# One more chunk of a weight product on ScalarE and two small copies on GpSimd in a graph network kernel

## What is computed

```python
def hyp_agg(x, src, dst, w, c, n_nodes):
    xt = logmap0(x, c)
    msg = xt[src] * w[:, None]
    agg = jax.ops.segment_sum(msg, dst, num_segments=n_nodes)
    return proj(expmap0(agg, c), c)
```

## Time and profile before

| | |
|---|---|
| Median of 3 runs | 1208.23 us (1206.75 to 1208.87) |
| The profiled execution, its own time | 1208.75 us |
| Its span, first to last instruction | 1206.9 us |
| TensorE busy | 1038.3 us (86%) |
| VectorE busy | 998.4 us (83%) |
| ScalarE busy | 668.8 us (55%) |
| GpSimd busy | 27.6 us (2%) |

### The profile page before, as it was taken

The page is one execution under the profiler, slowest core; times in us unless marked ns, Lnnn a source line. Parts: engine busy times, 40 slices in busy tenths (PEclk is TensorE's granted clock), DMA queues, the critical chain, the costliest instruction groups (busy, mean ns, idle before and its releaser), DMA issues.

```text
span 1206.9 us, 53493 instructions
## 1 busy us (share of the span) xinstructions
PE 1038.3 (86%) x22006; PEld 960.3 (80%) x22006; DVE 998.4 (83%) x1478; ACT 668.8 (55%) x1837; POOL 27.6 (2%) x28
## 2 busy tenths in 40 slices
PE   2079888898989898638996679999999999999997
PEld 2058778787777777437996569999999999999997
DVE  8889999999999999275665868888888888888884
ACT  5348888888888888310001565555555555555552
POOL 7000000000000000100000000000000000000000
PEclk9579999999999999859997779999999999999999
DMA  2002232323232322759940345444444444444440
GB/s 80 0 33 117 101 124 93 124 93 124 93 124 93 124 101 116 317 204 335 422 166 30 104 139 172 149 155 160 157 158 158 158 157 158 157 152 159 151 147 28
DMA packets 44875, 169.96 MB, mean 141 GB/s; under 512 B 19440, under 2 KB 19766, under 8 KB 44827
## 3 DMA queue, kind: packets, MB, share of 16 engines
q1 hardware_dynamic: 44827, 169.28, 38.7%
HBM read 121.11 MB, written 48.14 MB: 140 GB/s over the span
## 4 chain that ended last, share of the span: by engine, by line
PE 52%; DVE 33%; issue 8%; DVEq 4%; ACT 2%; DMA 0%; POOL 0%; POOLq 0%; ACTq 0%
PE PS L1507 17%; PE PS L1509 11%; PE PS L1382 8%; DVE arena L1008 7%; PE PS L1527 7%; DVE arena L985 5%; PE PS L1522 5%; DVE arena L993 4%; DVE arena L971 3%; DVE arena L980 2%; DVEq L354 2%; PE PS L1461 1%; PE PS L1413 1%; DVE Cw L799 1%; DVE rows L799 1%
## 5 line engine op out<-in xcount | busy, mean ns | idle before, releaser
L1507 PE MATMUL PS<-arena 125*128 125x128 bf16 x3600 | 343.8, 219 | 6.3 <-ACT RT L736 6.2
L1507 PEld LDWEIGHTS PS<-arena 125*128 125x128 bf16 x3600 | 249.9, 97 | 11.2 <-issue 6.9
L1382 PE MATMUL PS<-arena,A 125*64 125x72 f32 x4800 | 180.4, 231 | 72.3 <-DVE aggTw L1019 40.8
L1382 PEld LDWEIGHTS PS<-arena,A 125*64 125x64 f32 x4800 | 166.5, 139 | 81.7 <-issue 29.1
L631 ACT ACTIVATE arena<-arena 128x72 bf16<-128x72 bf16 x864 | 216.9, 343 | 2.1 <-DVE arena L993 2.1
L750 ACT ACTIVATE arena<-PS 128x512 bf16<-128x512 f32 (+2 forms) x336 | 171.9, 543 | 82.8 <-PE PS L1509 82.8
L743 ACT ACTIVATE arena<-arena 128x512 bf16<-128x512 f32 x144 | 90.8, 631 | 152.8 <-DVE arena L1226 152.7
L1509 PE MATMUL PS<-arena 108*128 108x128 bf16 x1200 | 166.9, 220 | 0.0
L1509 PE MATMUL PS<-arena,HTw 108*128 108x128 bf16 x1200 | 165.8, 219 | 0.0
L1367 PE MATMUL PS<-arena 128*128 128x72 bf16 x3600 | 126.7, 199 | 0.0
L1367 PEld LDWEIGHTS PS<-arena 128*128 128x128 bf16 x3600 | 120.7, 100 | 4.9
(11 more groups left out here) (189 smaller groups left out, 1340.0 us busy)
## 6 DMA issues: line engine op xcount, KB each, us to landing
adjacency<-arena SPq DMA_DIRECT2D x48, 900.0 KB, 3.6
arena<-adjacency SPq DMA_DIRECT2D x46, 900.0 KB, 7.6
Bw<-slot_rows SPq DMA_DIRECT2D x48, 800.0 KB, 4.1
Cw<-slot_rows SPq DMA_DIRECT2D x48, 700.0 KB, 4.3
arena<-q_table SPq DMA_DIRECT2D x144, 18.0 KB
q_table<-arena SPq DMA_DIRECT2D x6, 336.0 KB
slot_rows<-slot_row SPq DMA_DIRECT2D x49, 13.0 KB
x_sb<-in_x SPq DMA_DIRECT2D x1, 700.0 KB
```

The lines of the kernel that those rows point to most:

```text
L1382: last = mm(sums[half, :], A[:, b, :], adjacency[0:PN, b, :], start=(b < 2), stop=(b >= NB - 2))
L1507: mm(ps, OTs[k][:, b, :], P3[:, b, part, :], start=(part == 0), stop=False)
```

## The change

ScalarE multiplies the third weight part of all 25 buckets (25 instructions a group, before 18), and VectorE's product of 128x504 elements goes away. ScalarE no longer makes the two small copies out of PSUM; GpSimd makes them from `slots`, once `slots_set` is counted, and counts `copied`. `third_weights(g)` waits for `copied` of group g in place of `slots_set`. `third_set` counts four chunks a group where it counted three, and TensorE waits for it before each chunk.

```diff
+            def copy_slots(g, k):
+
+                pool.wait_ge(slots_set, nth(g))
+                if from_third(g):
+                    pool.wait_ge(third_set, nth(len(CHUNKS) * (g - 2) + len(CHUNKS) - 1))
+                nc.gpsimd.tensor_copy(slot_dst[:, bass.ds(g, 1), :, :].rearrange("p g b d -> p (g b) d"),
+                                      slots[k][:, 1, 0:NB, :])
+                nc.gpsimd.tensor_copy(third[k], slots[k][:, 4, 0:NB, 0]).then_inc(copied, 1)
+
+            fast = in_order(pool, 0)
+            with pool.If(fast == 1):
+                copy_slots(0, 0)
+                copy_slots(1, 1)
+                with pool.Fori(1, NG // 2) as j:
+                    copy_slots(2 * j, 0)
+                    copy_slots(2 * j + 1, 1)
@@ take_slots
                 sc.wait_ge(onehots_set, nth(g - 2))
-                nc.scalar.activation(slot_dst[:, bass.ds(g, 1), :, :].rearrange("p g b d -> p (g b) d"),
-                                     slots_ps[:, 1, 0:NB].unsqueeze(2).broadcast_to([128, NB, 2]), ACT.Copy)
-                nc.scalar.activation(third[k], slots_ps[:, 4, 0:NB], ACT.Copy)
+                sc.wait_ge(copied, nth(g - 2))
@@ third_weights
-                sc.wait_ge(slots_set, nth(g))
+                sc.wait_ge(copied, nth(g))
                 sc.wait_ge(dst1_set, nth(g))
                 sc.wait_ge(blocks_done[-1], nth(g - 2))
-                for bs in CHUNKS[1:]:
+                for bs in CHUNKS:
@@ slot_destinations
-                ve.wait_ge(third_set, nth(3 * g - 1))
+                ve.wait_ge(third_set, nth(len(CHUNKS) * g - 1))
@@ slot_weights
-                for c, n in ((2, CB), (0, NB), (1, NB)):
+                for c, n in ((0, NB), (1, NB)):
@@ blocks
-                    if c:
-                        pe.wait_ge(third_set, nth(3 * g + c - 1))
+                    pe.wait_ge(third_set, nth(len(CHUNKS) * g + c))
```

More of the change, by code:

```diff
@@ L274, in gnn_kernel @@
         dst1_set, onehots_set, third_set = counts("dst1_set"), counts("onehots_set"), counts("third_set")
+        copied = counts("copied")
         blocks_done, blocks_set = (counts(n, len(CHUNKS)) for n in ("blocks_done", "blocks_set"))
```

## The result

The change makes the kernel **slower**: 1292.31 us in the median of 4 runs (1285.94 to 1295.92) against 1208.55 for the kernel before in the same comparison (4 runs), a ratio of 1.068 with a 95% interval of 1.063 to 1.0736. The forecast was 1269, with a range of 1258 to 1300: right in direction and inside the range, 23 us too low at its middle. The profiled execution took 1295.92 us, its span is 1294.2, 87.3 more than before.

A forecast was written before the change was run, and what follows sets the result against it. VectorE (8.523 us a group) bounds the loop now; ScalarE would at 8.23 + 1.73 - 0.16 = 9.80. 46 groups add 58.7 us, the first interval 1.6: +60.3, about 1269 us, range 1258 to 1300.

The forecast's parts named there:

- forecast's own range: Range of the main case, ScalarE bounding the loop with hidden GpSimd copies: 1260 to 1278 us, chance 65%.
- GpSimd held twice: Rival, 15%: both GpSimd copies wait behind VectorE instructions, 3.5 us in all, 14 us more, about 1283 us.
- the clock: Rival, 5%: TensorE's clock falls through longer idleness, slowing blocks; 65 us more if each time, about 1334 us.
- ScalarE's circle: ScalarE's work and waits between runs of products in the loop: from 8.23 to 9.80 us a group, above VectorE's 8.19.
- Seven more products at 0.247 each: Added products on ScalarE in each loop group, between two engine answers: 1.73 us more a group.
- TensorE's new wait for the first chunk's products: TensorE's wait for third_set ahead of the first chunk of blocks: hidden, costs nothing.
- the sum: 58.7 us for 46 groups plus 1.6 for the first interval: +60.3 us on 1208.75, giving 1269.0 us.
- The copies on GpSimd: The two small copies in each group, ending about 1.7 us after the slots if held once: hidden, 0 us.
- cover: Time from the slots' copy to ScalarE's next products, in which GpSimd's copies can hide: 3.26 us.
- GpSimd gets in nowhere: Rival, 10%: GpSimd's copies get no turn until VectorE's add_sums; 101 us more, about 1370 us.
- The first copy: GpSimd's first copy, in the first group: 0.96 us extra once, covered by ScalarE's 2.06 us wait for VectorE.
- Not slower (3%): Rival, 3%: added ScalarE products overlap more deeply and cost little; 15.5 us less, about 1193 us.

The follow-up runs named there:

- kernel with the filled idle time: The changed kernel plus 24 unread 128x128 matrix products on TensorE between first_apply and slot_rows in each group; 1273.65 us (ratio 1.054).
- kernel with the copies alone: The kernel before with only the two small copies moved to GpSimd, ScalarE still multiplying 18 buckets and VectorE the first chunk; 1250.52 us (ratio 1.0331).
- kernel with the pause for GpSimd: The kernel with the copies alone, but VectorE's slot_destinations waits for GpSimd's copied of its own group instead of slots_set; 1228.20 us (ratio 1.0136).

## Why the prediction was right, and where it was short

- **Inside the range, in part by luck.** 1292.31 us lies outside the forecast's own range of 1260 to 1278. It lies inside 1258 to 1300 because that range had been widened for GpSimd held twice, a case whose 14 us did not come; the clock, whose case the range left out for the most part, took the room.
- **ScalarE's circle as the new bound: right, and exact.** Forecast 9.80 us, measured 9.82. *Seven more products at 0.247 each*: 25 take 6.13 from start to start (252.20 to 258.35 is 6.15), 0.245 each. The wait for `slot_rows` is 0.33 again, VectorE waits 1.40 us a group in front of `slot_destinations` where I had said 1.6, and TensorE's new wait for the first chunk's products shows in no row. The kernel with the filled idle time, where nothing disturbs the circle behind the first group, took 1273.65 in the median and 1271.53 in its profile: the forecast's 1269 was, to within 5 us, the change's price without the clock.
- **The clock: the step that failed.** In the sum it had 0, and as a rival 5%, with 65 us if it fell in each group "or if now and then, less". It fell now and then: 13 groups of about 1.53 us and the last of 1.57, 21.5 of the 27 us by which the profiled execution's 1295.92 exceeds the sum's 1269.0. The other 5.5 are 1.0 of GpSimd's hold in the first distance, 0.9 of 46 x 0.02, 0.3 ahead of the first run, and the 3.3 of the later layers. The kernel with the filled idle time shows it by taking it away: 19 us less. The mechanism and its price (1.38 against 1.53) were read from the right rows; its chance was not. I had idleness of 4.06 us with a fall and 0.82 without one, and put the new 2.1 us on the side of the second, with no row between. An honest reading would have given the case near a half and moved the middle up.
- **The copies on GpSimd: right in cost, by a margin that I had not seen.** I took one hold and 1.7 us; there were two, and 3.07 us of a cover of 3.35. The rival "held twice" had that mechanism, with 0.3 us for each copy's own time, 3.5 us, and so 14 us more. It had the turns right; but the copies' own time doesn't come on top of the holds, as each ends 0.06 to 0.08 us behind VectorE's instruction, so it came to nothing.
- **"GpSimd gets in nowhere"** is real, but not in the steady groups of this kernel: once, in the second group (a copy of 5.25 us, and 0.97 us of ScalarE's wait), and in 14 of 48 groups of the kernel with the copies alone. The Trainium skill (SBUF — State Buffer, Who interferes with whom) has whoever issues first block the other for its whole instruction. That is the hold of one instruction that most copies show (1.06 and 1.79 us); a copy of 6.05 us that waits through six instructions, of which only the first had started before it, goes beyond this rule, and the measurement decides.
- **The first copy**: 0.52 us in the first group, under VectorE, so the 0.96 that I allowed for it showed nowhere. The Trainium skill (GPSIMD Engine Reference, 2.1 Instruction dispatch) speaks of about 6 us for the first call to a freshly loaded kernel; they don't appear at this copy.
- **Not slower (3%)**: the products got no cheaper; it had no ground.

## What to carry to other kernels

Before giving work to the engine that looks idle, follow its own circle of waits: idle time between a request and its answer can be filled only by work placed between the two, and the changed kernel loses 84 us (some 20 of them the clock) with all 25 products in front of the request, and 18 with four of them behind it. When a new bound lengthens another engine's pauses, look whether TensorE's clock still holds; a row between a pause with a fall and one without is worth having before it is put at zero. And GpSimd's small copies out of SBUF are cheap only where VectorE pauses: if they stand behind a semaphore that a full VectorE does not wait for, price them at several of VectorE's instructions.

## What the runs showed of the hardware that I had not expected

TensorE's clock fell in 13 of 46 groups with pauses of 2.0 us in a circle of 9.8 (granted clock 0.59 over `blocks` in the one shown), in 9 of 46 with pauses of 2.2 in 10.0, and behind the first group never with pauses of 0.9 to 1.0 in 8.8, of 1.3 to 1.4 in 9.0 (the kernel with the pause for GpSimd) or of 0.6 in 9.8. What sets the groups with a fall apart from those without was not found out. And a GpSimd copy of 50 columns that takes 0.26 us beside a pausing VectorE took up to 7.6 us beside one that ran two-input instructions back to back, although VectorE passed several borders between instructions in that time; at which border GpSimd gets in differed from group to group and was not found out.
